# A GpSimd queue in another order: low halves of the rotation ahead of sums, and two sums a step later

## What is computed

```python
def _rope(x, base=ROTARY_BASE):
    ...
    even, odd = jnp.split(x, 2, axis=-1)
    return jnp.concatenate([even * cos - odd * sin, even * sin + odd * cos], axis=-1)
...
q = _rope(jnp.einsum('btm,mhd->bthd', x, w_aq))
k = _rope(jnp.einsum('btm,mhd->bthd', x, w_ak))
v = jnp.einsum('btm,mhd->bthd', x, w_av)
s = jnp.einsum('bihd,bjhd->bhij', q, k) / D_HEAD - INF_APPROX * mask
p = jax.nn.softmax(s, axis=-1)
r = jnp.einsum('bihd,hdm->bim', jnp.einsum('bhij,bjhd->bihd', p, v), w_ao)
...
x = _layernorm(x + r)
x = _layernorm(x + ffn(x))
```

## Time and profile before

| | |
|---|---|
| median of 3 runs | 1065.75 us (1064.59 to 1066.63) |
| the profiled execution | 1065.99 us, span 1064.2 us |
| attention in the span | to about 773 us |
| busy: TensorE | 997.1 us, 94% |
| busy: VectorE | 820.6 us, 77% |
| busy: ScalarE | 593.3 us, 56% |
| busy: GpSimd | 539.6 us, 51% |

### The profile page before, as it was taken

The page is one execution under the profiler, slowest core; times in us unless marked ns, Lnnn a source line. Parts: engine busy times, 40 slices in busy tenths (PEclk is TensorE's granted clock), DMA queues, the critical chain, the costliest instruction groups (busy, mean ns, idle before and its releaser), DMA issues. The chain is left out here.

```text
span 1064.2 us, 19686 instructions
## 1 busy us (share of the span) xinstructions
PE 997.1 (94%) x5648; PEld 860.2 (81%) x5648; DVE 820.6 (77%) x1803; ACT 593.3 (56%) x1255; POOL 539.6 (51%) x536
## 2 busy tenths in 40 slices
PE   3799999999999999999999999999839999999995
PEld 3688888898888889888888888888728878788784
DVE  5888888888888888887888888788555677486744
ACT  3566666665666666566666666666434252433521
POOL 4666767776676776677677666767250101000000
PEclk9899999999999999999999999999969999999998
DMA  8433233432322123323222222221020000000000
GB/s 282 150 127 74 61 80 97 124 99 56 75 69 69 49 59 100 70 61 79 59 49 59 61 70 68 72 59 40 1 80 1 1 1 21 1 20 0 1 20 21
DMA packets 33292, 66.16 MB, mean 62 GB/s; under 512 B 5457, under 2 KB 6993, under 8 KB 32209
## 3 DMA queue, kind: packets, MB, share of 16 engines
q1 hardware_dynamic: 30400, 58.62, 21.0%
q10 hardware_dynamic: 2832, 6.82, 1.7%
HBM read 24.26 MB, written 7.34 MB: 30 GB/s over the span
## 5 line engine op out<-in xcount | busy, mean ns | idle before, releaser
L703 POOL TENSOR_SCALAR probs<-probs,inv_sum 128x128 f32<-128x128 f32 (+7 forms) x256 | 191.1, 747 | 232.4 <-DVE inv_sum L621 231.8
L534 ACT ACTIVATE pT<-psum 128x512 fp32r<-128x512 f32 (+3 forms) x384 | 173.9, 490 | 144.0 <-PE psum L401 141.9
L308 PE MATMUL psum<-pT,vals 128*128 128x512 f32 (+3 forms) x1152 | 242.6, 351 | 1.6 <-DVE rT L663 1.6
L522 ACT ACTIVATE probs<-psum,neg_max 128x128 f32<-128x128 f32 (+7 forms) x256 | 190.5, 744 | 80.2 <-DVE neg_max L615 79.8
L615 DVE TENSOR_REDUCE neg_max<-psum 128x1 f32<-128x128 f32 (+7 forms) x256 | 191.2, 747 | 54.8 <-PE psum L392 53.6
L631 DVE TENSOR_TENSOR pT<-psum,pT 128x512 fp32r<-128x512 f32 (+3 forms) x384 | 200.7, 551 | 32.3 <-ACT pT L534 25.3
L308 PEld LDWEIGHTS psum<-pT,vals 128*128 128x128 f32 x1152 | 187.7, 189 | 23.9 <-DVE pT L631 1.7
L401 PE MATMUL psum<-ident,probs 128*128 128x128 f32 x1152 | 173.7, 277 | 12.9 <-POOL probs L703 12.2
L883 PE MATMUL ps<-hid,w 128*128 128x512 f32 x768 | 181.3, 396 | 0.0
L708 POOL TENSOR_TENSOR swapped<-by_cos,swapped 128x512 f32<-128x512 f32 x128 | 164.7, 1298 | 14.2 <-DMA swapped<-by_sin 14.2
L883 PEld LDWEIGHTS ps<-hid,w 128*128 128x128 f32 x768 | 143.7, 188 | 34.5
(11 more groups left out here) (77 smaller groups left out, 1195.3 us busy)
## 6 DMA issues: line engine op xcount, KB each, us to landing
swapped<-by_sin SPq DMA_DIRECT2D x256, 128.0 KB, 2.3
w_stage<-qk_split SPq DMA_DIRECT2D x30, 256.0 KB, 2.7
wv_stage<-v_split SPq DMA_DIRECT2D x15, 256.0 KB, 2.7
x_split<-ffn_raw ACTq DMA_DIRECT2D x2, 1024.0 KB, 5.8
ffn_raw<-g SPq DMA_DIRECT2D x2, 1024.0 KB, 8.0
x_moving<-x_split SPq DMA_DIRECT2D x2, 1024.0 KB, 5.1
out<-y SPq DMA_DIRECT2D x4, 512.0 KB, 2.6
raw_x<-xT SPq DMA_DIRECT2D x3, 512.0 KB, 11.6
```

Of the source, the lines that this page charges most:

```text
L308: ins = nc.tensor.matmul(out_ap, left[a], right[b], start=first and i == 0, stop=last and i == 2)
L522: nc.scalar.activation(probs[:, ib % 4, :width].rearrange("p (h c) -> p h c", h=halves), score_ps[:, ib % 2, :halves, :half], ACT.Exp, bia ...
L534: nc.scalar.activation(pT[chunk][:, 0, 4 * f:4 * f + n_blocks, (ib % 4) * P:(ib % 4 + 1) * P], bank("t", head[1], nth)[:, :n_blocks * P].r ...
L703: nc.gpsimd.tensor_scalar(p, p, inv_sum[:, n:n + 1], 1.0, ALU.mult, ALU.mult).then_inc(probs_ready[0], 1)
```

## The change

The sums of tiles three and four are queued a step later, in steps 5 and 6 instead of 4 and 5, and their high halves too, in steps 6 and 7 instead of 5 and 6. The low halves stay in steps 3, 4, 6 and 7. Within a step GpSimd takes low halves before sums instead of behind them; both occur in the same step only in step 4 before (sum of tile three, low half of tile two) and in step 6 after (low half of tile three, sum of tile four).

```diff
 QK_STEP = (0, 0, 2, 2)
-SUM_STEP = (2, 2, 4, 5)
-HIGH_STEP = (3, 3, 5, 6)
+SUM_STEP = (2, 2, 5, 6)
+HIGH_STEP = (3, 3, 6, 7)
 LOW_STEP = (3, 4, 6, 7)
...
                 if exists(ahead):
                     normalize(ahead, (s + 1) % NI)
+                for target, j in rope_tasks(head, s, LOW_STEP):
+                    roped_low(target, j)
                 for target, j in rope_tasks(head, s, SUM_STEP):
                     rope_sum(target, j)
-                for target, j in rope_tasks(head, s, LOW_STEP):
-                    roped_low(target, j)
```

## The result

The changed kernel takes **1127.05 us** (median of 4 runs, 1126.8 to 1128.07) against 1065.4 us before (4 runs), a ratio of 1.0579 with a 95% interval of 1.0565 to 1.0592: slower by 61.7 us. The forecast was 1121.3 us. The profiled execution took 1128.07 us with a span of 1126.3 us, 62.1 more than before.

What follows compares the result with a forecast made beforehand. TensorE was taken to bound the kernel, with almost no idle time in attention. 15 x 2.26 us in second heads plus 16 x 1.35 in first heads gave 55.5 us more, 1121.3 us, range 1102 to 1130.

Steps and rivals of the forecast that it cites:

- What bounds the kernel, and that every head makes the delay again: TensorE, busy 710.57 of 727 us in attention, bounds it; an unhidden delay in steps 6 and 7 recurs each head.
- Steps 4 and 5: Moving tile three's sum and high half, with tile two's low half earlier, gains and loses 0.
- Second head: Second head of a pair: ScalarE's copies of row block 7's transposes, and then TensorE, 2.26 us late, 15 times.
- First head: First head of a pair: the same ScalarE copies 1.35 us late, reaching TensorE's scores in full, 16 times.
- The lateness partly caught up: Rival: only TensorE's direct bank stalls count, not all of VectorE's lateness; 1102 us, chance 0.10.
- Absorbed: Rival: ScalarE's idle time absorbs the delay and TensorE stays fed; no change, 1066 us, chance 0.03.
- faster: Rival: emptier step 4 starts row block 6's normalization earlier, removing TensorE's 0.65 us wait in second heads; 1056 us, chance 0.04.
- T(6): TensorE's transposes of row block 6; the 0.65 us wait before them was to stay.
- rows 11: Start-up trace: a GpSimd sum took 2.26 us beside VectorE's two-SBUF-tile subtraction; such slowing would add 30 us in all.
- The clock: TensorE's granted clock should stay at its upper level in new gaps; rival with a fall or slowed sums: 1152+, chance 0.05.
- The start: The rotation before head 0, with TensorE mostly empty and waiting for VectorE's start-up work until 30 us, was given 0.
- The signs named: ScalarE's sum waits grow near 55 us; TensorE idle goes from 16 to about 72; first-projection wait 1.3 to 2 us.

Runs made afterwards that it cites:

- Order only: Kernel before with only GpSimd's order within a step changed, low halves ahead of sums: 1065.65 us, ratio 1.0002.
- high halves later: Kernel before with sums on time and only the high halves of tiles three and four a step later: 1065.68 us, ratio 1.0001.
- tile four alone: Changed kernel with tile three back in its old steps, low halves still first: 1129.28 us, ratio 1.0607.
- the start only: Kernel before with the later steps only for the rotation of heads 0 and 1: 1064.36 us, ratio 0.9988.

## Why the prediction was right, and where its size was off

*What bounds the kernel, and that every head makes the delay again*: right. Within each group of the table head times repeat to 0.1 us, but for one head of 25.15.

*Steps 4 and 5 at nothing*: right. Order only and high halves later only are at 1.000; tile four alone has the whole loss.

*Second head, 2.26*: measured 2.25 (mean of the 7 without a fall of the clock), with every link of the chain within 0.03 us. *First head, 1.35*: measured 1.35 (mean of 16). That the wait for the sum is the cause is shown from three sides: without it the same place costs nothing, with a shorter one the loss shrinks to 1.0 and 0.06, and with the copies ahead of it the loss falls to 1.05 and 0.29.

*The lateness partly caught up* (1102) did not happen: the full lateness reached TensorE. *Absorbed* and *faster* fell with it; the wait of 0.66 us before T(6) is still there (524.89 above), and GpSimd's sums kept their 1.29 us, so nothing was slowed in the way of rows 11. (The subtraction of rows 11 begins 1.27 us after that slow sum; the one beside its start is an earlier one, also of two SBUF tiles, in the timeline before:

```profile
23.42 2.30 DVE L590 TENSOR_TENSOR x_moving<-raw_x,x_moving 128x1024 fp32r<-128x1024 f32 x1
```

The reading, that such a subtraction slows a sum, stays.)

*The clock* is the step that failed. The prediction said that "the new gaps (2.1 us and less, with work all around) should keep the upper" level. It reasoned from one stretch with 4.60 us of work in 7 that kept it, and it treated a fall as all or nothing, 1152 or more. What happened is small and frequent: 8 falls in 15 gaps, 27.5 us in 8 heads instead of 8 x 2.25 = 18.0, so 9.5 us. Filling the gap took the falls and 8.6 us of the time away. That the time still lies within 1102 to 1130 is partly luck: the room above 1121 was meant for a longer delay in the first heads, which did not come.

*The start* was given 0 and gained 2.2 us in the profiled execution (N(6) of head 0 from 48.00 to 45.79): 1.0 by VectorE's earlier first maximum, the rest on the way from there to N(6), as the run with the start only shows.

The sum closes. Heads with N(6) as mark: 7 x 2.25 + 27.5 + 21.6 = 64.9; less 2.2 at the start and 0.6 behind the last N(6) (303.6 us before, 303.0 after) makes 62.1, the difference of the spans. The prediction had 55.5: the clock is 9.5 more, the start and the end 2.8 less.

*The signs named*: ScalarE's wait for the sums grew by 37.9 us in the window of rows 3, and over the whole span from 40.9 to 86.9 us, 46 instead of the 55 named: I had taken the lateness of the copies, which holds some of their own former waits. TensorE's idle time went to 787.00 - 731.60 = 55.4 us between 48 and 835 us and not to 72, and the wait before the first projection, named as 1.3 to 2 us, is 1.1 to 1.3:

```profile
48.00:835.00 787.00, 731.60 (x4368) 634.99 (x4366) 601.04 (x1239) 462.76 (x1058) 491.78 (x493) 0.98 0.25 64
```

Its recorded busy time rose by 21 us instead, some 10 of it at the lower clock. The rest, some 10 us in all or 0.3 us a head, I can't place; the ends of matmuls are modelled.

## What to carry to other kernels

When a producer is queued later, look first at the queue of its consumer: the instruction that now waits is the smaller harm, what stands behind it is the larger, and its consumers name the price. Whether such a wait is new is decided by the last hand-over alone, here 1.25 us of one low half in a queue without idle time, so two edits that cost 0 and 16 us alone can cost 62 together.

When a stall makes a gap of a microsecond on TensorE, price the clock as well, and not as all or nothing; a few transposes of no use in the gap show at once how much of the loss it is.

## What the runs showed of the hardware

- TensorE's granted clock fell to its lower level behind a third to a half of otherwise equal gaps (0.31 us of work in 1.40), at a cost of 1.2 us each; with three more transposes, the last wait 0.78 instead of 1.11 us, it fell behind none. Which of the equal gaps are hit was not found; it differs between the profiled executions of two kernels with the same gap (8 of 15 and 5 of 15).
- Beside a VectorE subtraction of two SBUF tiles, whichever engine is first by 0.1 us keeps its own time, and the other's instruction lasts 1 us longer: GpSimd's took 1.26 us when first and 2.23 us when second, VectorE's first subtraction 1.22 and 2.23 us. The Trainium skill (SBUF — State Buffer, Who interferes with whom) says that the port pair shared by the two is an exclusive lock, that a VectorE instruction with two SBUF inputs contends for it with a GpSimd instruction that reads SBUF, and that the order of issue decides who blocks; these traces agree.
